# A selective scan on one core: GpSimd takes 128 columns of the second sequence, and ScalarE's long stages are cut into parts

## The reference

```python
xn = x * rsqrt(mean(x * x) + 1e-6) * norm_w
xn = xn * sigmoid((xn @ select_proj_w.T + select_proj_b) * select_gate)
delta, B, C = split(xn @ x_proj_w.T)                       # 128 each
delta = softplus(delta @ dt_proj_w.T + dt_proj_b)
for t in range(1024):                                      # h: [2, 512, 128]
    h = exp(delta[t, :, None] * A) * h + (delta[t] * xn[t])[:, None] * B[t, None, :]
    y[t] = (h * C[t, None, :]).sum(-1)
x = layernorm(x + (y + x * D_param) @ out_proj_w.T)
x = layernorm(x + (silu(x @ w_gate.T) * (x @ w_up.T)) @ w_down.T)
```

## Time and profile before

| | us |
|---|---|
| median of 3 runs | 2693.13 (2690.42 to 2694.03) |
| profiled execution, its own time | 2687.74 |
| its span in the trace | 2685.9 |
| mean granted TensorE clock, share of full speed | 0.956 |

### The profile page before, as it was taken

One profiled execution on the slowest core, in us unless ns is written; L12 is line 12 of the kernel. 1 busy time (PEld: TensorE's weight loads), 2 busy tenths in 40 slices (PEclk: granted clock), 3 DMA queues, 4 the chain that ended last, 5 costly groups with the idle time before them and its releaser, 6 DMA issues.

```text
span 2685.9 us, 48350 instructions
## 1 busy us (share of the span) xinstructions
PE 2316.6 (86%) x17036; PEld 1290.5 (48%) x17036; DVE 2584.4 (96%) x4160; ACT 1708.6 (64%) x2229; POOL 1028.3 (38%) x1031
## 2 busy tenths in 40 slices
PE   7866678998789987899779997799977998899998
PEld 4322224554345543555345553455534554465567
DVE  6999999999999999999999999999999999999892
ACT  5687766667566665667656666566666667654643
POOL 2343333443434434344333443344333443344320
PEclk8999999999999989999889998899989999999899
DMA  4566665777667876678757786577866777788694
GB/s 171 197 213 227 228 236 211 281 277 270 237 223 277 284 266 223 238 275 292 254 195 247 279 290 243 201 267 277 278 241 209 279 279 271 239 289 308 228 357 151
DMA packets 192060, 672.16 MB, mean 250 GB/s; under 512 B 20944, under 2 KB 26064, under 8 KB 191824
## 3 DMA queue, kind: packets, MB, share of 16 engines
q1 hardware_dynamic: 152432, 544.02, 57.5%
q10 hardware_dynamic: 39392, 125.06, 13.3%
HBM read 660.61 MB, written 8.39 MB: 249 GB/s over the span
## 4 chain that ended last, share of the span: by engine, by line
PE 39%; DVE 28%; ACT 15%; issue 12%; DMA 6%; POOL 0%; ACTq 0%; DVEq 0%; POOLq 0%
DVE h L709 14%; PE banks L1200 11%; DVE banks L686 10%; PE banks L1036 10%; PE banks L1176 7%; PE banks L1276 7%; ACT a L981 6%; DVE h L706 4%; DMA u_bc<-u_scratch 4%; ACT L720 2%; DMA U<-in_xT 1%; PE banks L1128 1%; PE banks L1124 1%; ACT u_bc L1000 1%; ACT v L862 1%
## 5 line engine op out<-in xcount | busy, mean ns | idle before, releaser
L981 ACT ACTIVATE a<-banks 128x2048 f32<-128x2048 f32 x512 | 960.7, 1876 | 604.3 <-PE banks L1200 563.1
L686 DVE TENSOR_TENSOR banks<-a,h 128x512 f32<-128x512 f32 x2048 | 1324.1, 688 | 4.1 <-ACT a L981 4.1
L709 DVE SCALAR_TENSOR_TENSOR h<-u_bc,BCt,banks 128x512 f32<-128x512 f32 x1482 | 1038.2, 732 | 5.4 <-PE banks L1276 5.4
L581 POOL TENSOR_TENSOR dexp<-spread,dt 128x512 f32<-128x512 f32 x512 | 539.1, 1053 | 821.2 <-DVE banks L686 779.2
L1200 PE MATMUL banks<-dexp,A 32*128 32x256 f32 x8192 | 623.6, 421 | 150.6 <-ACT a L981 149.0
L1276 PE MATMUL banks<-h,cz 128*32 128x512 f32 x4096 | 667.9, 623 | 94.4 <-DVE h L706 64.7
L1200 PEld LDWEIGHTS banks<-dexp,A 32*128 32x128 f32 x8192 | 390.3, 195 | 484.4 <-ACT a L981 347.7
L1036 PE MATMUL banks<-vT,w_ring 128*128 128x256 f32 x1792 | 449.9, 394 | 7.6 <-ACT up L948 6.9
L1036 PEld LDWEIGHTS banks<-vT,w_ring 128*128 128x128 f32 x1792 | 323.8, 190 | 175.4 <-issue 118.2
L706 DVE TENSOR_TENSOR h<-u_bc,banks 128x512 f32<-128x512 f32 x566 | 367.5, 673 | 19.9 <-PE banks L1276 19.9
L593 POOL TENSOR_SCALAR u_bc<-u_bc,BCt 128x512 f32<-128x512 f32 x266 | 184.1, 692 | 404.6 <-DVE banks L686 394.3
(11 more groups left out here) (177 smaller groups left out, 1284.9 us busy)
## 6 DMA issues: line engine op xcount, KB each, us to landing
u_bc<-u_scratch SPq DMA_DIRECT2D x1021, 512.0 KB, 4.6
w_ring<-in_gu_w ACTq DMA_DIRECT2D x112, 512.0 KB, 5.5
w_ring<-in_down_w ACTq DMA_DIRECT2D x56, 512.0 KB, 5.7
a<-in_gu_w ACTq DMA_DIRECT2D x16, 512.0 KB, 12.7
a<-in_down_w ACTq DMA_DIRECT2D x8, 512.0 KB, 4.4
x_tok<-in_x_rows SPq DMA_DIRECT2D x15, 256.0 KB, 5.7
out_rows<-v ACTq DMA_DIRECT2D x15, 256.0 KB, 3.4
U<-in_xT ACTq DMA_DIRECT2D x7, 512.0 KB, 6.0
```

Source lines behind the costliest of these rows:

```text
L581: e.tensor_tensor(dexp[:, q % E_RING, :, :, :], spread[:, :].unsqueeze(1).unsqueeze(1).to_broadcast(shape), by_step[:, :, first:first + BS ...
L686: e.tensor_tensor(m_ps[:, b, :], a[:, blk % A_RING, b, s, :], h[:, (t - 1) % H_RING, b * D:(b + 1) * D], ALU.mult).then_inc(s_m, 1)
L709: e.scalar_tensor_tensor(h[:, t % H_RING, part], u_bc[:, t % U_RING, part], BCt[c % 2][:, 0, b * TB + tl:b * TB + tl + 1], m_ps[:, b, :], ...
L981: e.activation(dst.rearrange("p b t (x j) -> p x (b t) j", j=GP), src.rearrange("p g (i r j) -> p (g i) r j", i=PAIR, j=GP), ACT.Exp, scal ...
```

## The change

The last 128 channels (`SHARE`) of the second sequence go to GpSimd altogether. A new function `share(t)` does a step of them in three instructions: the product of `a` and `h` into a new tile `m_share`, the scaling of that part of `u_bc` by B in place, and their sum into `h`. VectorE's product and addition of the second sequence have 384 columns. The tables `on_pool` and `on_act` with both `scale` functions are gone, all 2048 additions of VectorE have the long form. GpSimd's waits on the products (`s_m`) ahead of dexp and of the pieces are gone too; its own semaphores `s_mg`, `s_zg`, `s_hg` count its products, scalings and sums, and SP, ScalarE and TensorE wait for them where they reuse or read what GpSimd has now a part in.

The squares, softplus and layer norms on ScalarE become two, three and two stages, each with its slot; gaps between some stages behind the scan differ. When two threads of the timetable are at the same slot, the one that was put off by the other comes later. The 128 x 128 matrix of 1/512 is now one column, broadcast.

```diff
-    yield from [("x_in", 0, 6), ("sq", 0, 4), ("ms", 0, 4), ("root", 0, 4)]
+    yield from [("x_in", 0, 6), ("sq", 0, 2), ("sq", 1, 2), ("ms", 0, 4), ("root", 0, 4)]
...
-        yield from [("dtp", j, 3), ("pre", j, 1), ("soft", j, 7), ("c1", j, 0), ("c2", j, 0), ("c3", j, 0), ("c4", j, 0)]
+        yield from [("dtp", j, 3), ("pre", j, 2), ("soft", 3 * j, 2), ("soft", 3 * j + 1, 3), ("soft", 3 * j + 2, 2), ("c1", j, 0), ("c2", j, 0), ("c3", j, 0), ("c4", j, 0)]
...
-        yield from [("outp", 2 * w, 3), ("outp", 2 * w + 1, 3 + wide), ("ln1", w, 2 * w if both else 4)]
+        yield from [("outp", 2 * w, 3), ("outp", 2 * w + 1, 3 + wide), ("ln1", w, 2 if both else 1), ("ln1b", w, 2 * w if both else 1)]
...
-        yield from [("back", w, 3 + wide), ("ln2", w, 1 + wide)]
+        yield from [("back", w, 3 + wide if x < LAST else 2), ("ln2", w, 1 + wide if x < LAST else 0), ("ln2b", w, 0)]
...
-        thread = min(threads, key=lambda t: t[0])
+        thread = min(threads, key=lambda t: (t[0], t[3]))
...
         if first and slot < emptied:
             thread[0] = emptied
+            thread[3] = emptied
             continue
...
                 if t >= U_RING:
                     e.wait_ge(s_h, BATCH * (t - U_RING + 1))
+                    e.wait_ge(s_hg, t - U_RING + 1)
                 e.dma_start(u_bc[:, slot, :], u_scratch[t, :, :].rearrange("b d -> (b d)").partition_broadcast(P)
                             ).then_inc(d_u[slot], 16)
...
+            def share(t):
+                c, blk, s, tl, slot = t // TB, t // BS, t % BS, t % TB, t % U_RING
+                part, of_b = slice(BATCH * D - SHARE, BATCH * D), slice(D - SHARE, D)
+                if s == 0:
+                    e.wait_ge(s_exp, 2 * (blk + 1))
+                if t:
+                    e.wait_ge(s_hg, t)
+                e.tensor_tensor(m_share[:, :], a[:, blk % A_RING, 1, s, of_b], h[:, (t - 1) % H_RING, part], ALU.mult
+                                ).then_inc(s_mg, 1)
+                if t < FIRST_U:
+                    e.wait_ge(s_ucp, BATCH * (t + 1))
+                else:
+                    e.wait_ge(d_u[slot], 16 * (t // U_RING + (slot >= FIRST_U)))
+                if t == 0:
+                    e.wait_ge(s_bc, 1)
+                elif tl == 0:
                     e.wait_ge(s_work, emptied("xp", c, 0))
+                e.tensor_scalar(u_bc[:, slot, part], u_bc[:, slot, part], BCt[c % 2][:, 0, TB + tl:TB + tl + 1], 1.0, ALU.mult,
+                                ALU.mult).then_inc(s_zg, 1)
+                if t >= H_RING:
+                    e.wait_ge(s_y, t - H_RING + 1)
+                e.wait_ge(s_mg, t + 1)
+                e.wait_ge(s_zg, t + 1)
+                e.tensor_tensor(h[:, t % H_RING, part], m_share[:, :], u_bc[:, slot, part], ALU.add).then_inc(s_hg, 1)
...
             for t in range(SEQ):
                 c = t // TB
+                share(t)
                 if t in DEXP_AT:
-                    e.wait_ge(s_m, BATCH * (t + 1))
                     diagonals(DEXP_AT[t])
                 if t % 2:
                     for slot in range(SLOTS * (t % TB - 1), SLOTS * (t % TB + 1)):
                         for stage, x, j in plans[c].get(slot, ()):
-                            if stage in PIECES:
-                                e.wait_ge(s_m, BATCH * (t + 1))
                             piece_before(e, x, stage, j)
                             piece_behind(e, x, stage, j)
-                    if (t + 1, 0) in on_pool:
-                        e.wait_ge(s_m, BATCH * (t + 1))
-                        scale(t + 1)
...
-                    e.tensor_tensor(m_ps[:, b, :], a[:, blk % A_RING, b, s, :],
-                                    h[:, (t - 1) % H_RING, b * D:(b + 1) * D], ALU.mult).then_inc(s_m, 1)
+                    e.tensor_tensor(m_ps[:, b, 0:cols], a[:, blk % A_RING, b, s, 0:cols],
+                                    h[:, (t - 1) % H_RING, b * D:b * D + cols], ALU.mult).then_inc(s_m, 1)
...
+                    part = slice(b * D, b * D + width(b))
+                    e.scalar_tensor_tensor(h[:, t % H_RING, part], u_bc[:, t % U_RING, part],
+                                           BCt[c % 2][:, 0, b * TB + tl:b * TB + tl + 1], m_ps[:, b, 0:width(b)], ALU.mult,
+                                           ALU.add).then_inc(s_h, 1)
...
-                    product(dst[:, 0:TC], [(mean_mat[:, :], T[:, k, :]) for k in range(KB)]).then_inc(s_ms, 1)
+                    product(dst[:, 0:TC], [(mean_col[:, :].to_broadcast([P, P]), T[:, k, :]) for k in range(KB)]).then_inc(s_ms, 1)
...
                 if blk >= A_RING:
                     e.wait_ge(s_m, BATCH * BS * (blk - A_RING + 1))
+                    e.wait_ge(s_mg, BS * (blk - A_RING + 1))
...
                 e.wait_ge(s_h, BATCH * (t + 1))
+                e.wait_ge(s_hg, t + 1)
```

More of the change, by code:

```diff
@@ L29 @@
 U_RING = 5
+SHARE = 128
 E_RING = 4
@@ L359, in build @@
         turns, norms = {}, {}
-        def at_steps(t, steps):
-            return [(stage, j) for step in range(max(t, 0), t + steps) for slot in (SLOTS * (step % TB), SLOTS * (step % TB) + 1)
-                    for stage, _, j in plans[step // TB].get(slot, ())]
-        def light(t):
-            return sum(LOAD.get(stage, 0) for stage, _ in at_steps(t, 2)) <= LIGHT
-        def quiet(t):
-            return t < TB or t < LAST * TB and 88 <= t % TB < 112
-        even = range(FIRST_Z, SEQ - 4, 2)
-        on_pool = {(t + 2, 0): i for i, t in enumerate(
-            t for t in even if not any(stage in PIECES for stage, _ in at_steps(t, 2)))}
-        on_act = {place: i for i, place in enumerate(
-            place for t in even if quiet(t) and light(t) and light(t - 2) for place in ((t + 2, 1), (t + 3, 0), (t + 3, 1)))}
         for c in range(CHUNKS + 1):
@@ L678, in vector, with width @@
             e.wait_ge(s_utc, BATCH)
+            def width(b):
+                return D - SHARE if b else D
             for t in range(SEQ):
@@ L992, in window @@
                 last.then_inc(s_ycp, 1)
-            def scale(t, b):
-                c, tl, slot = t // TB, t % TB, t % U_RING
-                if tl < 4 and c:
-                    e.wait_ge(s_work, emptied("xp", c, 0))
-                e.wait_ge(d_u[slot], 16 * (t // U_RING + (slot >= FIRST_U)))
-                part = u_bc[:, slot, b * D:(b + 1) * D]
-                e.activation(part, part, ACT.Copy, scale=BCt[c % 2][:, 0, b * TB + tl:b * TB + tl + 1]).then_inc(s_za, 1)
             first_chunk()
@@ L1016, in scalar @@
                         exponents(EXP_AT[SLOTS * t + i], p_ps)
-                    if i == t % 2:
-                        for place in ((t + 2, 0), (t + 2, 1)):
-                            if place in on_act:
-                                scale(*place)
                     for stage, x, j in plans[c].get(SLOTS * (t % TB) + i, ()):
@@ L1213, in first_chunk @@
                 e.wait_ge(s_sqv, 1)
-                product(ms_first, [(mean_mat[:, :], T[:, k, :]) for k in range(KB)]).then_inc(s_ms, 1)
+                product(ms_first, [(mean_col[:, :].to_broadcast([P, P]), T[:, k, :]) for k in range(KB)]).then_inc(s_ms, 1)
                 e.wait_ge(d_wsel, 16)
```

139 lines of the change are left out of this document (69 added, 70 removed).

## The result

| | us |
|---|---|
| before, median of 4 | 2691.8 (2683.3 to 2694.0) |
| after, median of 4 | 3189.8 (3186.9 to 3191.3) |
| ratio | 1.186, interval 1.183 to 1.188 |
| after, span of the profiled execution | 3185.1 |

The change makes the kernel 18.6% slower. The direction was forecast, and so was the cause, products and GpSimd's instructions that exclude each other; the size was not: 2960 us was named, with a range up to 3150.

The account below looks back on a forecast made before the run. VectorE was taken to bound the kernel before at 2.52 us a step, GpSimd after at 2.79. Ahead 38.4, scan 2856, behind 65.4, plus 1.8 around the span and 5 to the median: 2967, named 2960 us, range 2700 to 3150.

Parts of the forecast that it names:

- What bounds the kernel before: In the scan, VectorE's instruction stream, 96% busy, sets the end at 2.52 us for each of 1024 steps.
- rivals 1 and 2: Faster: engines interleave and only held times add, 2665 us, 8%; or no exclusion, VectorE alone sets 2425 us, 5%.
- A product and a GpSimd instruction exclude each other: VectorE's 512-column product holds 0.53 us, GpSimd's instruction all but its last 0.13; the waiting one enters at the next boundary.
- VectorE alone, 2.26 us a step: VectorE's products and additions, the second sequence's narrowed by 128 columns, undisturbed: 2314 us for the scan.
- GpSimd's three instructions: GpSimd's share each step: product and addition of 128 columns at 0.46 us each, scaling at 0.31.
- The holds: VectorE's four products in two steps hold 1.86 us; slipping in between costs GpSimd 1.2 of it.
- A piece adds 1.2 us: A 512-column GpSimd piece, in at most every second step, adds 1.2 us; 226 during the scan, 271 us.
- 0, ends -15 and +15: ScalarE's layer norm, softplus and squares in new slots: no change in time, between -15 and +15 us.
- Why VectorE can't run on: Waits for u_bc's five buffers, y rows and `a` leave GpSimd some three steps of lag, then its pace is everyone's.
- Rival 4: Slower still: the hold lasts to the instruction's end, or waits cost 0.3 us in place of 0.14; 3180 us, 10%.
- The removed waits: On GpSimd, no wait on products is left ahead of its work; counted within the two-step sum, without its own size.
- The signs that were named: Right if: products far above 688 ns, GpSimd over 80% busy, dexp well over 1.05, VectorE waiting, chunk 0 0.2 us quicker.

Follow-up runs that it names:

- e3: The kernel after, with VectorE's product taking its second input from PSUM in place of h in SBUF from the second step on: 2701 us, ratio 1.003.
- e10: The kernel after without GpSimd's share, its waits on VectorE's products put back, ScalarE's stages in one piece and the old timetable: 2615 us, ratio 0.972.
- e1: The kernel after without GpSimd's share (those 128 channels stay zero), GpSimd's waits on VectorE's products put back: 2699 us, ratio 1.003.
- e4: The kernel after, with GpSimd's scaling of u_bc written as a two-input product with a broadcast column of B: 3122 us, ratio 1.160.
- e7: The kernel before, without GpSimd's waits on VectorE's products ahead of dexp, the pieces and its scalings: 3046 us, ratio 1.132.
- e12: The kernel after, with GpSimd's waits on the same step's products put back ahead of dexp and the pieces: 3188 us, ratio 1.185.

## Why the prediction was wrong, by its own steps

**What bounds the kernel before** (VectorE, 2.52 us a step): right, but half of it. TensorE was not looked at stage by stage. Its mean of 2.2 us a step was set against 2.79 and found harmless, which was enough for the forecast. For rivals 1 and 2 it was not: without any exclusion (e3) the time is 2701 and not 2425, since TensorE holds the dense stretches of a chunk at up to 3 us a step, and VectorE, with six buffers of h, can't run ahead of them in the light ones. With the change's timetable, nothing that took away the exclusion or the share came below 2699; with the old one, e10, which has no share at all, is at 2615, 2.8% below the kernel before.

**A product and a GpSimd instruction exclude each other:** right; e3 shows it directly, since nothing but the place of the product's second input differs. The release 0.13 us early and the 0.53 us of hold were borne out at 1002.10 and 1004.60.

**VectorE alone, 2.26 us a step:** right: 0.687 + 0.554 + 0.741 + 0.606 in e3, less the usual overlaps, and 2.25 us a step in e1's light stretch (18.04 us for 8 steps).

**GpSimd's three instructions:** product and addition were named at 0.46 and took 0.457 and 0.456. The scaling was named at 0.31 and took 0.37. Together 1.285 in place of 1.23, 56 us. The gap ahead of the addition was put at 0.14 and is 0.18 (182.9 us of idle time over 1024), but the one ahead of a product that directly follows an addition is 0.11; less 0.12 of overlaps, gaps add 0.345 to two steps where the sum had 0.32 (3.83 - 2.46 - 1.05): 13 us.

**The holds:** here is the failing step. "Four VectorE products hold ... 1.86 ... I take 1.2" for two steps, 0.60 a step. Measured, GpSimd loses 0.77 - 0.46 = 0.32 at m_share and 0.80 - 0.37 = 0.43 at the scaling, and hardly anything elsewhere: 0.75 a step, 1.5 for two and not 1.2, which makes 0.15 x 1024 = 154 us. Dexp, at 1.070 for 1.049, adds 11 us. I had let every GpSimd instruction slip in at the next boundary, since rows 9 and 10 showed two-input instructions doing so. That is where it fails: in the kernel after, 272 one-input scalings waited for both products. Each is held 0.83 us, where the 269 of e4 that go between are held 0.39, and 0.44 x 272 = 120 of the 154 us. In the two-input form (e4), itself dearer, that is gone, and 68 us of the total with it. The rest is not split further.

**A piece adds 1.2 us:** it adds 1.08. By the starts of m_share, two steps without a piece take 5.49 us in the mean, where the sum had 5.03, and two with a piece 6.57: 0.12 x 226 = 27 us less.

Together 56 + 13 + 154 + 11 - 27 = 207 of the scan's 3069 - 2856 = 213 us. Behind the scan, "nothing else is changed" and "0, ends -15 and +15" for ScalarE's parts were wrong: 3185.1 - 3106.2 = 79 us in place of 65, by the y rows that come late. The change itself shortens gaps there (stages "back" and "ln2").

**Why VectorE can't run on:** right in outcome, wrong in the way. VectorE waited 15.9 us for u_bc and 4.3 for y rows in the whole run. By these rows what ties it to GpSimd's pace is the products themselves: both engines lose 0.7 us a step in the same meetings, VectorE (1.195 + 0.764) - (0.687 + 0.554) = 0.72, GpSimd 0.75.

**Rival 4** had a time near the measured one (3180) for reasons that are not borne out: the hold does not last to the instruction's end, and the wait costs 0.18, not 0.3.

**The removed waits** were counted into the sum and not priced alone. In the kernel before they are worth 357 us (e7), but e12 shows that putting them back into the kernel after gives nothing.

**The signs that were named:** products at 1195 ns in the mean and up to 1.63 us, GpSimd at 90%, and chunk 0 at 2.86 us a step against 3.02 in the middle chunks all came. Dexp "at well over 1.05" did not: it takes 1.07, as it starts beside the additions, and it is the products that wait for it. Nor did VectorE's waits for u_bc and y rows, 20 us.

## What to carry to other kernels

Before work is moved to GpSimd beside a saturated VectorE, count which VectorE instructions read two inputs from SBUF; a GpSimd instruction that meets them costs both engines, so it has to fit in the windows between them (here 1.3 us a step, with the kernel before using most of it). Where GpSimd waits for "the other engine's products are done", that wait may be the most valuable line of the kernel, and it protects nothing where GpSimd comes to it late, half-way through the additions (e12), or has another wait behind it (e1). And before pricing a gain, run the second engine's stretches one by one: this kernel's first bound is 96% busy in the mean, and once it was relieved (e1) the next one stood at 92% in the dense stretches.
